# A graph convolution's counting sort on one core: ranks taken as marked minima, and ScalarE scaling the embeddings' products

## The reference

```python
def gcn_conv(x, W, b, row, col, num_nodes):
    h = x @ W
    loop = jnp.arange(num_nodes)
    row_sl, col_sl = jnp.concatenate([row, loop]), jnp.concatenate([col, loop])
    deg = segment_sum(ones_like(col_sl), col_sl, num_nodes)
    dinv = rsqrt(maximum(deg, 1.0))
    msg = h[row_sl] * (dinv[row_sl] * dinv[col_sl])[:, None]
    return segment_sum(msg, col_sl, num_nodes) + b

h1 = gcn_conv(emb, W1, b1, row, col, 25000)      # 64 -> 128 features
lookup = gcn_conv(h1, W2, b2, row, col, 25000)   # 128 -> 64 features
return lookup[r_input]
```

## Time and profile before

| | us |
|---|---|
| median of 3 runs | 6993.59 |
| lowest and highest run | 6985.06, 7000.94 |
| the profiled execution | 6975.57 |
| its span in the trace | 6973.8 |

### The profile page before, as it was taken

One profiled execution on the slowest core, in us unless ns is written; L12 is line 12 of the kernel. 1 busy time (PEld: TensorE's weight loads), 2 busy tenths in 40 slices (PEclk: granted clock), 3 DMA queues, 4 the chain that ended last, 5 costly groups with the idle time before them and its releaser, 6 DMA issues.

```text
span 6973.8 us, 133704 instructions
## 1 busy us (share of the span) xinstructions
PE 5035.2 (72%) x27034; PEld 4251.7 (61%) x27035; DVE 4284.9 (61%) x14137; ACT 2098.6 (30%) x6145; POOL 4543.0 (65%) x4733
## 2 busy tenths in 40 slices
PE   6858788888888888899788888888888888100000
PEld 5633355755655665799788888888888888100000
DVE  8988899899889889767566555555555555000000
ACT  7957666566566566511100000000000011000000
POOL 0000377767767767777677777777777777677777
PEclk9989999899899999855555555555555555555555
DMA  0001111111111111111111111111111111111111
GB/s 14 0 18 39 27 25 25 27 21 25 26 21 25 26 20 25 26 36 41 37 26 26 26 26 26 26 26 26 26 26 26 34 39 39 45 53 53 53 53 52
DMA packets 184476, 210.96 MB, mean 30 GB/s; under 512 B 81356, under 2 KB 100182, under 8 KB 184336
## 3 DMA queue, kind: packets, MB, share of 16 engines
q0 software_dynamic: 151040, 154.97, 11.3%
q1 hardware_dynamic: 15280, 35.45, 1.3%
q10 hardware_dynamic: 18016, 19.05, 0.9%
HBM read 163.62 MB, written 45.54 MB: 30 GB/s over the span
## 4 chain that ended last, share of the span: by engine, by line
PE 34%; POOL 25%; issue 19%; DVE 14%; DMA 6%; DVEq 3%; ACT 0%; POOLq 0%; SPq 0%; ACTq 0%
PE ps L656 24%; POOL scratch L371 14%; POOL acc L404 11%; PE ps L561 9%; DMA scratch<-table,source 5%; DVE late L1016 3%; DVE place_i L994 3%; DVE acc L1037 2%; DVE hi_onehot L829 2%; DVE late L1027 1%; DVE picked L988 1%; PE ps L709 1%; DVE prt_onehot L829 0%; DVEq L1035 0%; DVEq L1027 0%
## 5 line engine op out<-in xcount | busy, mean ns | idle before, releaser
L371 POOL DMA_INDIRECT scratch<-table,source x3920 | 3785.5, 966 | 2154.1 <-issue 1104.5
L656 PEld LDWEIGHTS ps<-scratch,late 128*128 128x128 f32 x19520 | 3685.6, 283 | 766.2 <-issue 643.7
L656 PE MATMUL ps<-scratch,late 128*128 x19520 | 3723.5, 368 | 455.6 <-SPq L336 259.6
L1037 DVE TENSOR_TENSOR acc<-acc,ps 128x128 f32 x4880 | 1357.8, 278 | 1250.9 <-PE ps L656 1225.9
L1027 DVE TENSOR_SCALAR late<-ramp,target 128x256 f32<-128x256 f16 x4392 | 1654.2, 377 | 162.1 <-issue 95.0
L457 ACT ACTIVATE late<-prt_onehot,scratch 125x128 f16<-125x128 f16 x4000 | 1214.7, 387 | 699.6 <-DVE prt_onehot L829 600.0
L561 PE MATMUL ps<-late 125*128 125x488 f16 x4000 | 1125.1, 372 | 164.6 <-DVE late L1016 164.5
L404 POOL DMA_INDIRECT acc<-lookup,scratch x800 | 754.7, 943 | 267.4 <-issue 243.5
L533 ACT ACTIVATE acc<-acc,dinv (+1 forms) x196 | 57.5, 340 | 2441.9 <-DVE acc L1037 2441.9
L1016 DVE TENSOR_SCALAR late<-ramp,tcol 125x488 f16<-125x488 f16 x2000 | 685.0, 350 | 0.0
L561 PEld LDWEIGHTS ps<-late 125*128 125x128 f16 x4000 | 363.7, 113 | 314.7 <-DVE late L1016 203.7
(11 more groups left out here) (145 smaller groups left out, 1079.1 us busy)
## 6 DMA issues: line engine op xcount, KB each, us to landing
scratch<-table,source POOLq DMA_INDIRECT x3920, 2.5
out<-acc SPq DMA_DIRECT2D x40, 640.0 KB, 3.0
acc<-lookup,scratch POOLq DMA_INDIRECT x800, 2.4
table<-acc SPq DMA_DIRECT2D x49, 128.0 KB, 2.5
table<-acc ACTq DMA_DIRECT2D x49, 128.0 KB
lookup<-acc ACTq DMA_DIRECT2D x49, 128.0 KB
late<-embT ACTq DMA_DIRECT2D x47, 128.0 KB, 2.7
scratch<-edge_index SPq DMA_DIRECT2D x2, 976.6 KB
```

The costliest lines, as they stand in the source:

```text
L371: pool.indirect_dma_start(out=place, out_offset=None, in_=table[r], in_offset=bass.IndirectOffsetOnAxis(ap=source[:, t:t + 1], axis=0)).th ...
L656: last = pe.matmul(visit_ps[odd * W8 + k][:, n * FEAT:(n + 1) * FEAT], target_onehot[:, odd * W8 + k, n * P:(n + 1) * P], row, start=True, ...
L1037: dve.tensor_tensor(dst, dst, visit_ps[odd * W8 + k].rearrange("p (n f) -> p n f", f=FEAT), ALU.add).then_inc(visits_added, 1)
```

## The change

1. *The marks.* The triangle `before` gets -65536 on its diagonal (`MARK`), a triangle `after` gets +65536 there, and a mask `itself` has ones on the diagonal only. `rank_before` thus lowers an edge's own entry by 65536, and the place is the minimum over the 98 blocks, read by one reduction straight from PSUM (`least_ranks`); `cut_places` drops the mark by its mask and shift. `pick_ranks` and the tile `picked` are gone. The masks and `blk_onehot` are BF16 instead of FP16.
2. *The rest.* `rank_rest` becomes four matmuls: two with `after` (which takes the mark away) and two with `itself`. It stands behind column 1 instead of column 0 in the sort's batches, and behind the third visit and column instead of the first in the combined ones.
3. *The steps* per batch in `rank_step` are 5 instead of 6, and the list `BOTH` loses its "pick"; "least" stands where "sum" stood.
4. *The scaling.* DVE's instruction of line 1124 is gone. ACT scales the four tiles one by one, behind the pieces of columns 4, 5, 6 and 7; `emb_scaled` counts tiles.
5. `sign_half` gets a buffer of its own.

The diff, cut:

```diff
-            pool.affine_select(out=not_before[:, :], in_=ones[:, :], compare_op=ALU.is_ge, fill=0.0,
+            pool.affine_select(out=after[:, :], in_=ones[:, :], compare_op=ALU.is_gt, fill=0.0,
                                base=0, pattern=[[-1, P]], channel_multiplier=1).then_inc(triangles_made, 1)
+            pool.affine_select(out=itself[:, :], in_=ones[:, :], compare_op=ALU.is_equal, fill=0.0,
+                               base=0, pattern=[[1, P]], channel_multiplier=-1).then_inc(triangles_made, 1)
+            pool.wait_ge(triangles_made, 3)
+            for triangle, mark in ((before, -MARK), (after, MARK)):
+                pool.affine_select(out=triangle[:, :], in_=triangle[:, :], compare_op=ALU.not_equal, fill=float(mark),
+                                   base=0, pattern=[[1, P]], channel_multiplier=-1).then_inc(triangles_made, 1)
...
-            def sort_batch(i, k, load):
+            def sort_batch(i, k, load, scale=True):
...
                         act.wait_ge(emb_multiplied, s + 1)
                         act.dma_start(emb_sb[:, b, :], embT[:, bass.ds((s + 2) * EN, EN)]).then_inc(emb_loaded[b], 16)
+                    if scale and j >= W8 - ET:
+                        n = j - (W8 - ET)
+                        act.wait_ge(emb_multiplied, s + 1)
+                        act.activation(acc[:, bass.ds(s * ET + n, 1), :].rearrange("p a f -> p (a f)"),
+                                       emb_ps[b][:, n * FEAT:(n + 1) * FEAT], ACT.Copy,
+                                       scale=dinv[:, bass.ds(s * ET + n, 1)]).then_inc(emb_scaled, 1)
...
             def rank_rest(s):
                 pe.wait_ge(rank_step, s * RANK + 1)
-                for h in range(2):
-                    last = add(rank_ps[:, h, :], not_before[0:EP, :], halves[0:EP, h, :])
+                for counted_by in (after, itself):
+                    for h in range(2):
+                        last = add(rank_ps[:, h, :], counted_by[0:EP, :], halves[0:EP, h, :])
                 last.then_inc(rank_advanced, 1)
...
                 place_column(s, 0)
-                rank_rest(s + 1)
                 place_column(s, 1)
+                rank_rest(s + 1)
                 pe.wait_ge(emb_loaded[b], i * 16 + 16)
-                pe.wait_ge(emb_scaled, s + 1)
+                pe.wait_ge(emb_scaled, s * ET + ET)
...
-                    if more and k == 0:
+                    if more and k == 2:
                         rank_rest(s + 1)
...
-            def pick_ranks(s):
+            def least_ranks(s):
                 dve.wait_ge(rank_summed, s + 1)
-                dve.tensor_tensor(picked[E, :, :].rearrange("p (h j) n -> p h (j n)", h=2), rank_ps[E, :, :],
-                                  blk_onehot[E, :, :].rearrange("p (h j) n -> p h (j n)", h=2), ALU.mult).then_inc(rank_step, 1)
-            def sum_ranks(s):
-                dve.wait_ge(rank_step, s * RANK + 1)
-                    dve.tensor_reduce(place_i[E, 0, :], picked[E, :, :], AX.X,
-                                      ALU.add).then_inc(rank_step, 1)
+                    dve.tensor_reduce(place_i[E, 0, :].rearrange("p (h j) -> p h j", h=2),
+                                      rank_ps[E, :, :].rearrange("p h (j n) -> p h j n", n=NB), AX.X,
+                                      ALU.min).then_inc(rank_step, 1)
...
                 column_onehot(s, 0, b)
-                pick_ranks(s + 1)
                 column_onehot(s, 1, b)
-                sum_ranks(s + 1)
+                least_ranks(s + 1)
                 column_onehot(s, 2, b)
...
-                if emb:
-                    dve.wait_ge(emb_multiplied, s + 1)
-                    dve.tensor_tensor(acc[:, bass.ds(s * ET, ET), :], emb_ps[b].rearrange("p (t f) -> p t f", f=FEAT),
-                                      dinv[:, bass.ds(s * ET, ET)].unsqueeze(2).broadcast_to([P, ET, FEAT]),
-                                      ALU.mult).then_inc(emb_scaled, 1)
...
-BOTH = [("blocks",), ("target", 0), ("column", 0), ("late add", 4), ("target", 1), ("pick",), ("late add", 5), ("column", 1),
-        ("target", 2), ("sum",), ("late add", 6), ("column", 2), ("cut",), ("late add", 7), ("column", 3), ("load",),
+BOTH = [("blocks",), ("target", 0), ("column", 0), ("late add", 4), ("target", 1), ("late add", 5), ("column", 1),
+        ("target", 2), ("least",), ("late add", 6), ("column", 2), ("cut",), ("late add", 7), ("column", 3), ("load",),
```

More of the change, by code:

```diff
@@ L81 @@
 assert 3 * EC <= HISTW + CHUNKS * SLOTS <= RINGT * FEAT - SLOTS and RINGT <= P and CHUNKS * GB * P < 1 << 15
+assert CV * P < MARK and MARK // P % RW == 0
 assert CB % 2 == 0 and GROUPS == CB - 1 and LOOPED * STEPS + 4 == CB - 2
@@ L120, in build @@
         ones = sb("ones", [P, P], F16)
-        before = sb("before", [P, P], F16)
-        not_before = sb("not_before", [P, P], F16)
+        before = sb("before", [P, P], BF16)
+        after = sb("after", [P, P], BF16)
+        itself = sb("itself", [P, P], BF16)
         hi_onehot = sb("hi_onehot", [P, 2, W8, NT], F16)
@@ L160, in build @@
         visits = sb("visits", [2, CHUNKS * CV], I32)
-        blk_onehot = sb("blk_onehot", [P, W8, NB], F16)
-        picked = sb("picked", [P, W8, NB], F32)
+        blk_onehot = sb("blk_onehot", [P, W8, NB], BF16)
         place_i = sb("place_i", [P, 2, W8], I32)
@@ L287, in build @@
         GATHERS = CHUNKS * GB
-        RANK = 6
+        RANK = 5
         DEC = 9
@@ L413, in twice @@
                                 digits[0:EP, :].unsqueeze(2).broadcast_to([EP, EC, 2]))
+            act.sem_inc(emb_scaled, 2 * ET)
             act.wait_ge(ints_made, 7)
@@ L719, in place_batch @@
                     place_column(s, j)
-                    if j == 0:
+                    if j == 1:
                         rank_rest(s + 1)
@@ L984, in block_onehots, with cut_places, cast_places @@
                            edge_hi[E, bass.ds(s * (2 * W8), 2 * W8)].rearrange("p (j r) -> p j r", r=2)).then_inc(blk_onehots, 1)
-            def pick_ranks(s):
+            def least_ranks(s):
                 dve.wait_ge(rank_summed, s + 1)
-                dve.tensor_tensor(picked[E, :, :].rearrange("p (h j) n -> p h (j n)", h=2), rank_ps[E, :, :],
-                                  blk_onehot[E, :, :].rearrange("p (h j) n -> p h (j n)", h=2), ALU.mult).then_inc(rank_step, 1)
-            def sum_ranks(s):
+                with nc.allow_low_precision(reason="a whole number"):
+                    dve.tensor_reduce(place_i[E, 0, :].rearrange("p (h j) -> p h j", h=2),
+                                      rank_ps[E, :, :].rearrange("p h (j n) -> p h j n", n=NB), AX.X,
+                                      ALU.min).then_inc(rank_step, 1)
+            def cut_places(s, b):
                 dve.wait_ge(rank_step, s * RANK + 1)
-                with nc.allow_low_precision(reason="one whole number among zeros"):
-                    dve.tensor_reduce(place_i[E, 0, :], picked[E, :, :], AX.X,
-                                      ALU.add).then_inc(rank_step, 1)
-            def cut_places(s, b):
+                dve.tensor_scalar(place_i[E, 1, :], place_i[E, 0, :], P - 1, None, ALU.bitwise_and).then_inc(rank_step, 1)
+                dve.tensor_scalar(tcol[E, b, :], place_i[E, 0, :], 7, RW - 1, ALU.logical_shift_right,
+                                  ALU.bitwise_and).then_inc(rank_step, 1)
+            def cast_places(s):
                 dve.wait_ge(rank_step, s * RANK + 2)
-                dve.tensor_scalar(place_i[E, 1, :], place_i[E, 0, :], P - 1, None, ALU.bitwise_and).then_inc(rank_step, 1)
-                dve.tensor_scalar(tcol[E, b, :], place_i[E, 0, :], 7, None, ALU.logical_shift_right).then_inc(rank_step, 1)
-            def cast_places(s):
-                dve.wait_ge(rank_step, s * RANK + 3)
                 dve.tensor_copy(prt16[E, :, :], place_i[E, 1, :].unsqueeze(2).broadcast_to([EP, W8, 2])).then_inc(rank_step, 1)
             def partition_onehots(s, b):
-                dve.wait_ge(rank_step, s * RANK + 5)
+                dve.wait_ge(rank_step, s * RANK + 4)
                 dve.wait_ge(pieces_ready, s * (2 * W8) + (PIECE_CREDIT - 2 * W8))
@@ L1101, in first_places @@
                 block_onehots(s)
-                pick_ranks(s)
-                sum_ranks(s)
+                least_ranks(s)
                 cut_places(s, 0)
@@ L1108, in _, with sort_batch @@
             first_places(0)
-            def sort_batch(i, k, emb=True):
+            def sort_batch(i, k):
                 s, b = i * STEPS + k, k % 2
@@ L1137, in _ @@
             seed_ranks(1)
-            sort_batch(*divmod(CB - 1, STEPS), emb=False)
+            sort_batch(*divmod(CB - 1, STEPS))
             decode(0)
@@ L1143, in _ @@
             for s in range(CB, CB + AHEAD):
-                sort_batch(*divmod(s, STEPS), emb=False)
+                sort_batch(*divmod(s, STEPS))
             dve.wait_ge(visits_loaded, 16)
@@ L1168, in both @@
                         block_onehots(s + 1)
```

(6 more changed lines are left out.)

12 lines of the change are left out of this document (6 added, 6 removed).

## The result

The changed kernel takes 6901.91 us (median of 4 runs, 6898.20 to 6904.83) against 6996.85 us (4 runs, 6985.06 to 7000.94) for the kernel before on the same chip: ratio 0.9867, 95% interval 0.9850 to 0.9884, so 1.3% faster. The forecast was 6904.

A forecast was written before the change was run, and what follows sets the result against it. The sort-and-visits cycle bounded the first layer's chunks, POOL's gathers the second layer. Long waits -95 and first chunk +5 gave -90 on 6975.6, so 6886; from the median 6993.6, 6904 us, range 6868 to 6956 (8 in 10).

The forecast's parts named there:

- Long waits of POOL, -95 us: First layer's gathers: POOL's waits of 30.1, 30.7 and 34.2 us for a ring place would go, 95 us together.
- The combined batch, 9.46 to 8.35 us: Sort beside visits: without the pick and its wait, DVE's batch falls from 9.46 to 8.35 us; PE needs 7.85.
- the estimated limit of 8.8 us: Sort beside visits: any combined batch up to 8.8 us, a loss of 0.64, leaves POOL's 516 us per chunk the longer.
- BF16 block one-hots at no cost: DVE's block one-hots, FP16 in and BF16 out: 0 taken, between bounds of 0 and +0.41 us per batch.
- The first chunk, +5 us: First chunk's sort with scalings on ACT: 6.8 us per batch against 6.67, 49 x 0.1 = 5 us slower.
- the chain's 6.6 to 7.0: First chunk's batch: embeddings' matmuls, ACT's scalings and pieces, column 7, rank pair, minimum, rest: a period of 6.6 to 7.0 us.
- The excess per gather: Combined stretches: gathers take 1.317 us each against 1.263 alone; the excess of 0.054, per batch, should stay.
- rival C: Combined stretches: denser DVE hinders POOL's gathers; at double excess 80 us over 1500 gathers, net -10, 6984 us; chance 0.06.
- the 1.33 named as the sign of a wrong forecast: Profile after: gathers above 1.33 us would show the forecast wrong.
- Rivals A: First chunk: ACT's activations don't overlap, 8.2 us per batch, 75 us slower, net -20, 6974 us; chance 0.07.
- B: Combined batches: a batch drops only 0.4 us, so the gain is 61 us, 6933 us; chance 0.10.
- D: Minimum reads PSUM slowly: 1.7 us cancels the combined batches' gain, past about 2.1 ends slower, 7053 us; chance 0.04.

The follow-up runs named there:

- the ranks alone: Changed kernel with the scaling left on DVE ahead of the partition one-hots: 9194.38 us against 9265.24 of the kernel before, on a pausing chip, ratio 0.9922.

## Why the prediction was right

- *Long waits of POOL, -95 us.* Right in mechanism and size. They went (at most 0.3 us left), they came back (51 us) when the batch was made 9.04 us long, and at 8.6 us they stayed away, on either side of the estimated limit of 8.8 us.
- *The combined batch, 9.46 to 8.35 us.* It is 8.20 to 8.25: the minimum at 1006.31, 1014.51, 1022.76 and 1030.96 us. The minimum takes 0.968 us on the mean of 250 (0.975 taken).

```profile
L1007 DVE TENSOR_REDUCE place_i<-ps 125x8 int32<-125x784 f32 x250 | 241.9, 968 | 110.6 <-PE ps L578 110.5
...
L846 DVE TENSOR_TENSOR blk_onehot<-ramp,scratch 125x784 bf16<-125x784 f16 x250 | 139.4, 558 | 6.3 <-issue 5.1
```

- *BF16 block one-hots at no cost.* 558 ns against 561: right, and with it the page on errata in the Trainium skill that the forecast weighed ("Advanced Engine Details and Errata", 2x-1p requirements): FP16 in and BF16 out keeps the fast rate.
- *The first chunk, +5 us.* It was -6.9: 12 us better, inside the range of -28 to +25. The batch is 6.61 us, at the lower end of the chain's 6.6 to 7.0. The terms that were too large are the scalings and the DMA issue on ACT, for which 0 to 0.4 us stood in the sum: with its wait already met it costs 0.08. The scalings from PSUM took 0.302 us in the median of 196, against the 0.34 of the row from SBUF; the 0.04 between them is what the errata table of "VectorE: DVE Perf Modes" in the Trainium skill gives. That the saving on DVE is worth nothing here held too: the ranks alone had the same first gather, to 0.1 us. That ACT's place in the chain has a price stood in the prediction as the 28 us between 6.67 and a batch of 6.1 with a quick ACT; what it didn't ask is whether another place in the stream would earn them. It does, and more: moved behind column 7, or to DVE behind column 5, 34 to 36 us against the changed kernel.
- *The excess per gather.* Here a step failed. Against rival C the prediction said that "the other DVE instructions of a batch stay as they are, and so should the excess per batch". The distance rose from 1.303 to 1.316 us, and 1960 x 0.013 = 25 us of the 95 went back that way. It stayed under the 1.33 named as the sign of a wrong forecast over the first layer, and was just over it in the combined stretches (1.333). C's direction came true at a third of its price (25 of 80 us), but not by a denser DVE as such: one more DVE instruction within SBUF per batch should then cost, and the stream became 27 us shorter. Of the lock told of in "SBUF — State Buffer" of the Trainium skill ("Who interferes with whom") this case shows the part on copies: a gather that meets one within SBUF is lengthened (1.175 us), one that meets a copy from PSUM isn't (0.945). Counting locks, as the rival did, points the right way for these copies (20 us) and the wrong way for the sum. Whether such a lock makes the single gather 1.42 us long, next to the partition one-hots, isn't settled.
- *The sum.* Between the profiled executions -77 us, forecast -90: the 12 us of the first chunk one way, the 25 us of the gathers the other. That the median still met the forecast within 2 us is partly luck: the profiled execution of before lay further under its median than the one of after.
- *Small slips in the sums.* The low end of the range took 3 us for the spread of the runs before where the text has 8 and the lowest run lies 8.5 under the median, so it should be 6863; and 9.46 - 0.89 - 0.25 + 0.02 is 8.34. Neither bears on the outcome.
- Rivals A (ACT's sum of 8.2 us per batch), B (a batch that loses 0.4 us) and D (a minimum of 1.7 us or more) are out by the batch of 6.61, the batch of 8.20 and the 0.968 us.

## What to carry to other kernels

Where an engine is shared by a producer and a ring, work out how long its cycle may be before the ring runs full; any saving beyond that point buys nothing, and here some 8.8 us (an estimate, with 8.6 and 9.04 measured on its two sides) would have done where 8.2 was reached. When work moves to a spare engine, ask what stands behind it in that engine's stream and whose chain that is: the scaling's time on DVE or ACT cost nothing here, its place 36 us. And when an engine's loop is shortened, look at how its new period falls on the engine beside it: the mean of an instruction there can move without any change in the load.

## What was not expected of the hardware

- A DVE copy of 0.55 to 0.59 us within SBUF, added to each combined batch, made the kernel 25 us faster in the spans, though it lengthens the gathers that it meets (6869.33 against 6901.91 us in the medians; each beside its own kernel before, 0.9827 against 0.9867).
- The granted clock in the stretch 1374 to 1800 us fell from 0.99 to 0.94 with PE busier, at no visible cost. Busy us as above, then granted clock:

```profile
1374.00:1800.00 426.00, 388.32 (x2574) 299.05 (x2573) 378.03 (x1343) 304.52 (x907) 324.48 (x319) 0.94 0.13 25
```

- The same program takes 6.9 ms on some chips and 9.2 on others, with pauses of 5 to 17 us of PE, DVE and ACT once the gathers run, and slower gathers where POOL works alone. Its cause is open.
